# Node one-hots of a graph kernel's edge passes: made by ScalarE, two groups ahead, in place of VectorE

## The chip, the cores and the metric

The kernel runs on one core of a Trainium2 chip. The metric is the device time in microseconds (us) of one execution, the median of several.

## What is computed

The reference is two layers of a graph network with 3125 nodes of 256 features and 50000 edges, sorted by target node. Each layer adds a graph attention block and a mixing block, and then a mixture of experts. Only the edge passes matter here. The first layer has two of them (one head), the second has one (eight heads). A pass is, in short:

```python
xl = x @ Wl
xr = x @ Wr
xj = xl[src]
h = leaky_relu(xj + xr[dst] + eattr @ We, 0.2)
logits = h @ att
m = segment_max(logits, dst)
ex = exp(logits - m[dst])
alpha = ex / segment_sum(ex, dst)[dst]
out = segment_sum(xj * alpha[:, None], dst)
```

The pass with eight heads takes its logits from three sums per edge and head in place of `h @ att`.

## The kernel before

**Tiles.** Nodes lie in 25 tiles of P = 125 partitions. The edges are cut by a plan, made once at the start, into S = 432 steps. A step holds up to 125 edges whose targets lie in one node tile. G = 16 steps are a group, and a pass runs over NG = 27 groups. `messages` (line 641) is one pass; it is called for the two passes with one head (line 3095) and for the one with eight (line 3138). They are called pass 1, 2 and 3 here.

**One step.** GpSimd gathers the source rows of the step's edges by one indirect DMA (L733). TensorE makes `xr[dst]` as a product of a one-hot matrix with the node tile: the one-hot matrix `oht` has nodes along the partitions and edges along the free dimension (`score`, L939; L949 with eight heads). With one head a second product adds the gathered row (L943), and VectorE takes relu, the weights `att` and the sum in one instruction (`relu`, L778). For the sums by target there is the other one-hot matrix, `oh`, with edges along the partitions (`aggregate`, L985), and VectorE adds each product to the accumulator (`combine`, L869).

**The two one-hot matrices.** `oh` is made by ScalarE (`edge_hots`), one step at a time: the distance of an iota from the edge's target (L1037), then relu(1 - distance) (L1041), 32 instructions a group. `oht` starts as a broadcast: SP loads the targets of the group's 2000 edges into all 125 partitions (L750), and with one head the two edge attributes into two more rows (L752). Then one VectorE instruction per group compares all of it with the partition's own number (`node_hots`, L773) in place, and sets `oht_ready`, for which TensorE waits at the first score of the group. The buffer has RB = 3 slots.

**Softmax.** Per group the logits are turned (`turn_logits`, L956), scanned for maxima by VectorE, and the ends, carries and maxima go through TensorE four more times (L961, L968, L974, L979). VectorE's `arguments` (L837 to L843) releases ScalarE's Exp (`weights`, L1027) and TensorE's `spread_factor` (L979). With one head ScalarE scales the 16 gathered rows (L1048); with eight heads VectorE does that (L850).

**The order of the work.** Each engine runs a sequence written out by hand, and semaphores join them. In body j TensorE takes scores of group j+1 and sums of group j-1 in turn, in eight pairs of steps, with the five turns of group j behind pairs 0 to 4. VectorE goes through k = 0 to 15: relu of group j+1, combine of group j-1, and between them `own_maxima` (k = 1), `carries` (3), `maxima` (5), `arguments` (8); at k = 9 stand `node_hots` for group j+2 and `take_sources` (L142), which hands the source numbers of group j+3 to GpSimd. With eight heads `scale` follows at k = 12 to 15. The body ends with `logits` of group j+1. ScalarE's body j is Exp, scales, the factor (L1031), and `edge_hots` of group j+1. SP loads the `oht` of group j+3 when the scores of group j are done and the maxima of group j are ready. GpSimd gathers group g in four blocks, each behind the sums of that block of group g-3.

**The start of a pass.** VectorE makes the first three `take_sources`, then node_hots of groups 0 and 1, then clears the accumulator (L902). ScalarE begins with `edge_hots` of group 0.

Of the kernel before, what the change touches and what calls it, by code (L numbers as in the profile page):

```python
# [15 lines left out]
ALU = mybir.AluOpType  # L16
ACT = mybir.ActivationFunctionType
# [3 lines left out]
P = 125  # L21
# [7 lines left out]
NG = S // G  # L29
RB = 3  # L30
# [109 lines left out]
def copy_ts(nc, out, in_):  # L140

    return nc.vector.tensor_scalar(out, in_, 1.0, None, ALU.mult)  # L142
# [498 lines left out]
def messages(nc, name, call, c, table, heads, dst_rows, edge_lin, att, acc, marks, ee):  # L641
# [12 lines left out]
    with Stage(nc, name) as st:  # L654
# [3 lines left out]
        oht = st.sb("oht", [K1, RB, G * P])  # L658
# [27 lines left out]
        hots_landed = [st.sem(f"hots_landed{q}") for q in range(RB)]  # L686
        pens_landed = [st.sem(f"pens_landed{q}") for q in range(RB)]
        oh_ready = st.sem("oh_ready")
        oht_ready = st.sem("oht_ready")
        dist_ready = st.sem("dist_ready")  # L690
        z_ready = st.sem("z_ready")
        z_used = st.sem("z_used", credit=3)
        lg_ready = st.sem("lg_ready")
# [14 lines left out]
        hots_in = 48 if one else 32  # L708
        loops = (NG - 3) // RB

        def at_steps(g, n=G):
            return bass.ds(g * G, n)
# [8 lines left out]
        with st.block() as block:  # L721
# [43 lines left out]
            def _(dve):  # L765
                ch = Chain(dve, order)

                def take_sources(g, u):
                    copy_ts(nc, cur[:, u % RB, :], c.src_s[:, at_steps(g)]).then_inc(slot_ready.sem, 1)

                def node_hots(g, u, lap):
                    dve.wait_ge(hots_landed[u % RB].sem, hots_landed[u % RB].at(lap * hots_in + hots_in))
                    nc.vector.tensor_scalar(oht[0:P, u % RB], oht[0:P, u % RB], c.part[0:P, 0:1], None, ALU.is_equal).then_inc(oht_ready.sem, 1)  # L773

                def relu(g, u, k):
                    if k % 2 == 0:
# [75 lines left out]
                def node_tiles(g, half):  # L852
                    return load_row(nc, mybir.EngineType.DVE, c.nt_row[0:1, bass.ds(g * G + half * (G // 2), G // 2)], NT)

                def rescale(g, u, nt):
                    dve.wait_ge(fac_ready.sem, fac_ready.at(g + 1))
                    dve.wait_ge(combined.sem, combined.at(g * G))
                    if one:
                        a_t = acc[:, bass.ds(nt, 1), 0:W].rearrange("p a f -> p (a f)")
                        ch(nc.vector.tensor_scalar(a_t, a_t, fac[:, u % RB, 0:1], None, ALU.mult))  # L860
                    else:
                        a_t = acc[:, bass.ds(nt, 1), :].rearrange("p a (h f) -> p (a h) f", h=heads)
                        ch(nc.vector.tensor_tensor(a_t, a_t, fac[:, u % RB].unsqueeze(2).broadcast_to([P, heads, dr + 1]), ALU.mult))
# [7 lines left out]
                def body(j, u, i, first=False, final=False, spare=True):  # L871
                    nts = None
                    for k in range(G):
                        if not first and k % (G // 2) == 0:
                            nts = node_tiles(j - 1, k // (G // 2))
                        if not first and k == 0:
                            rescale(j - 1, u - 1, nts[0])
                        if one and not final:
                            relu(j + 1, u + 1, k)
                        if not first:  # L880
                            combine(j - 1, u - 1, k, nts[k % (G // 2)])
                        if k == 1:
                            own_maxima(j, u, i + u // RB)
                        if k == 3:
                            carries(j)
                        if k == 5:
                            maxima(j, u)
                        if k == 8:
                            arguments(j, u)
                        if k == 9 and not final and spare:  # L890
                            node_hots(j + 2, u + 2, i + (u + 2) // RB)
                            take_sources(j + RB, u)
                        if not one and k in (12, 13, 14, 15):
                            scale(j, u, k - 12)
                    if not final:
                        logits(j + 1, u + 1, i + (u + 1) // RB)

                for q in range(RB):
                    take_sources(q, q)
                node_hots(0, 0, 0)  # L900
                node_hots(1, 1, 0)
                ch(nc.vector.memset(acc[:], 0.0))  # L902
                nc.vector.memset(carry[:], -BIG)
                ch(nc.vector.memset(ends_row[:], -BIG))
# [118 lines left out]
            @block.scalar  # L1023
            def _(act):
                def weights(g, u):
                    act.wait_ge(arg_ready.sem, arg_ready.at(g + 1))
                    nc.scalar.activation(ex[:, u % RB], arg[:], ACT.Exp).then_inc(ex_ready.sem, 1)  # L1027

                def factors(g, u):
                    act.wait_ge(facp_ready.sem, facp_ready.at(g + 1))  # L1030
                    nc.scalar.activation(fac[:, u % RB], facp, ACT.Exp).then_inc(fac_ready.sem, 1)  # L1031

                def edge_hots(g, u):

                    for k in range(G + 1):
                        if k < G:
                            nc.scalar.activation(dist[:, k % 4, :], c.iota[0:P, 0:P], ACT.Abs, scale=-1.0, bias=c.rel[:, bass.ds(g * G + k, 1)]).then_inc(dist_ready.sem, 1)  # L1037
                        if k == 0:
                            continue
                        act.wait_ge(dist_ready.sem, dist_ready.at(g * G + k))  # L1040
                        last = nc.scalar.activation(oh[:, u % RB, k - 1, :], dist[:, (k - 1) % 4, :], ACT.Relu, scale=-1.0, bias=c.ones[0:P, 0:1])  # L1041
                    last.then_inc(oh_ready.sem, 1)

                def scale(g, u, k):
                    if k == 0:
                        act.wait_ge(ex_ready.sem, ex_ready.at(g + 1))
                    r = rows[:, u % RB, k, 0:W]
                    nc.scalar.activation(r, r, ACT.Copy, scale=ex[:, u % RB, k:k + 1]).then_inc(scaled.sem, 1)  # L1048

                def body(j, u, final=False):  # L1050
                    weights(j, u)
                    if one:
                        for k in range(4):
                            scale(j, u, k)
                    factors(j, u)
                    if one:
                        for k in range(4, G):
                            scale(j, u, k)
                    if not final:
                        edge_hots(j + 1, u + 1)  # L1060

                edge_hots(0, 0)
                body(0, 0)
                for i in range(loops):
                    for u in range(1, RB + 1):
                        body(i * RB + u, u)
                body(NG - 2, NG - 2)
                body(NG - 1, NG - 1, True)

# [2148 lines left out]
```

## Time and profile before

| | us |
|---|---|
| runs (three) | 5356.63, 5372.47, 5395.53 |
| median | 5372.47 |
| profiled execution | 5395.91 |
| its span | 5394.1 |
| TensorE matmul busy | 4372.8 (81%) |
| VectorE busy | 2810.2 (52%) |
| ScalarE busy | 2150.7 (40%) |
| GpSimd busy | 1957.3 (36%) |

The profile is one execution. PE is TensorE's matmuls, PEld its weight loads, DVE is VectorE, ACT is ScalarE, POOL is GpSimd, SP is SyncE and SPq its queue. L773 is line 773 of the kernel. Times are in us from the start of the span unless marked ns. "<-" behind an idle time names what ended it; "issue" is time in which an engine waited for nothing that the profile shows. The clock of TensorE is given as a share of 2.4 GHz. A float32 matmul of the program is two instructions. The three edge passes lie at about 1604 to 2330, 2546 to 3265 and 3930 to 4670 us.

### The profile page before, as it was taken

The numbers are of one execution on the slowest core, as the hardware profiler recorded it, in microseconds if no ns is written. First come the engines' busy times: TensorE is split into PE (matmuls) and PEld (weight loads), VectorE is DVE, ScalarE is ACT, GpSimd is POOL, SyncE is SP. The second block draws the span as 40 slices with busy tenths as digits, with TensorE's granted clock in tenths as the row PEclk, the third lists the DMA queues.
The fourth block names the chain that finished last, engine by engine and source line by source line (L and its number), as shares of the span: only waits on it lengthen the run. The fifth ranks groups of instructions, "written<-read, shape, count | busy, mean of one in ns | idle before, by whom it ended". The sixth has DMA issues, their size and how long they took to land. (4 is left out here: it accounts for less than half of the span.)

```text
span 5394.1 us, 74052 instructions
## 1 busy us (share of the span) xinstructions
PE 4372.8 (81%) x22063; PEld 3643.8 (68%) x22064; DVE 2810.2 (52%) x8470; ACT 2150.7 (40%) x6545; POOL 1957.3 (36%) x1544
## 2 busy tenths in 40 slices
PE   9499999999968989986889998389468888556694
PEld 9379888797856777754677775379346666345694
DVE  2262542626316666634666663643547677628424
ACT  2244434445334566623466662323433343121222
POOL 0000000000008777701887771056268888200141
PEclk9799999999989999967999996589656666677697
DMA  5510000000025555412555543632666666210613
GB/s 136 155 43 1 17 10 18 10 1 17 10 67 124 125 125 123 113 39 51 120 130 123 121 112 72 173 113 69 135 139 133 137 139 133 68 43 5 212 35 85
DMA packets 371044, 469.79 MB, mean 87 GB/s; under 512 B 166216, under 2 KB 303417, under 8 KB 370208
## 3 DMA queue, kind: packets, MB, share of 16 engines
q1 hardware_dynamic: 178964, 264.68, 19.4%
q0 software_dynamic: 191744, 200.92, 17.1%
q8 instruction: 175, 2.87, 0.2%
q14 instruction: 161, 1.32, 0.1%
HBM read 399.94 MB, written 63.87 MB: 86 GB/s over the span
## 5 line engine op out<-in xcount | busy, mean ns | idle before, releaser
L733 POOL DMA_INDIRECT msg_rows<-tab_d,msg_cur x1296 | 1646.0, 1270 | 1781.5 <-DVE msg_cur L142 1361.3
L985 PE MATMUL msg_agp<-msg_rows,msg_oh 125*125 125x261 f32 (+2 forms) x2592 | 848.5, 457 | 15.4 <-DVE ga_acc L869 7.0
L985 PEld LDWEIGHTS msg_agp<-msg_rows,msg_oh 125*125 125x125 f32 x2592 | 548.1, 223 | 128.3 <-issue 22.6
L939 PE MATMUL msg_zp<-g_xr,msg_oht 127*125 x1728 | 547.2, 398 | 80.4 <-DVE msg_oht L773 63.3
L943 PE MATMUL msg_zp<-msg_rows,c_ident 125*125 125x256 f32 x1728 | 527.0, 386 | 37.4 <-DMA msg_rows<-tab_d,msg_cur 37.4
L778 DVE SCALAR_TENSOR_TENSOR msg_hid<-msg_zp,g_att 125x256 f32<-125x256 f32 x864 | 360.5, 420 | 316.0 <-PE msg_zp L943 208.4
L1037 ACT ACTIVATE msg_dist<-c_iota,c_rel 125x125 f32<-125x125 f32 x1296 | 493.0, 387 | 48.8 <-PEq L3020 33.9
L1041 ACT ACTIVATE msg_oh<-msg_dist,c_ones 125x125 f32<-125x125 f32 x1296 | 493.2, 387 | 0.0
L1027 ACT ACTIVATE msg_ex<-msg_arg 125x16 f32<-125x16 f32 (+1 forms) x81 | 20.0, 247 | 1020.7 <-DVE msg_delta L843 829.3
L869 DVE TENSOR_TENSOR gv_acc<-gv_acc,msg_agp 125x261 f32 (+1 forms) x864 | 364.3, 422 | 104.4 <-PE msg_agp L985 69.7
L939 PEld LDWEIGHTS msg_zp<-g_xr,msg_oht 127*125 127x125 f32 x1728 | 307.9, 190 | 136.5 <-issue 85.7
L943 PEld LDWEIGHTS msg_zp<-msg_rows,c_ident 125*125 125x125 f32 x1728 | 328.7, 191 | 97.8 <-DMA msg_rows<-tab_d,msg_cur 43.9
L1317 PE MATMUL mix_pb<-mix_ht,mix_w 128*128 128x125 f32 x3200 | 373.5, 275 | 0.0
L1326 PE MATMUL mix_pc<-mix_w,mix_ut 128*125 128x256 f32 x1600 | 361.8, 380 | 7.0 <-ACT mix_ut L1458 7.0
L1317 PEld LDWEIGHTS mix_pb<-mix_ht,mix_w 128*128 128x128 f32 x3200 | 365.6, 192 | 0.4
L1048 ACT ACTIVATE msg_rows<-msg_rows,msg_ex 125x257 f32<-125x257 f32 x864 | 354.2, 497 | 1.7
L1593 DVE TENSOR_TENSOR mix_t<-mix_pc,mix_b 125x256 f32<-125x256 f32 x100 | 42.4, 424 | 543.5 <-PE mix_pc L1326 543.5
L1326 PEld LDWEIGHTS mix_pc<-mix_w,mix_ut 128*125 128x125 f32 x1600 | 292.9, 188 | 47.9 <-issue 8.3
L1279 PE MATMUL mix_pb<-mix_wp,mix_ht 128*125 128x256 f32 x1200 | 282.7, 387 | 4.1 <-ACT mix_ht L1398 4.1
L869 DVE TENSOR_TENSOR ga_acc<-ga_acc,msg_agp 125x264 f32 x432 | 184.4, 427 | 161.0 <-PE msg_agp L985 129.8
L1279 PEld LDWEIGHTS mix_pb<-mix_wp,mix_ht 128*125 128x125 f32 x1200 | 222.6, 192 | 36.4 <-issue 5.5
L1398 ACT ACTIVATE mix_ht<-mix_pa,mix_gb 128x125 f32<-128x125 f32 x208 | 82.8, 450 | 369.2 <-PE mix_pa L1268 369.2
(540 smaller groups left out, 7258.9 us busy)
## 6 DMA issues: line engine op xcount, KB each, us to landing
msg_oht<-rel_d SPq DMA_DIRECT2D x81, 875.0 KB
msg_rows<-tab_d,msg_cur POOLq DMA_INDIRECT x1296
pl_raw<-in_edge_attr SPq DMA_DIRECT2D x25, 448.0 KB
msg_pens<-pen_d SPq DMA_DIRECT2D x270, 31.2 KB
msg_oht<-rel_d SPq DMA_DIRECT2D x81, 101.6 KB
mix_w<-in_L_mix_W SPq DMA_DIRECT2D x8, 1024.0 KB
m0w_wr<-in_L_ffn_w SPq DMA_DIRECT2D x16, 512.0 KB
m0w_w2r<-in_L_ffn_w SPq DMA_DIRECT2D x16, 512.0 KB
```

Source lines behind the costliest of these rows:

```text
L733: nc.gpsimd.indirect_dma_start(out=rows[:, q, k, :], out_offset=None, in_=table, in_offset=bass.IndirectOffsetOnAxis(ap=cur[:, q, k:k + 1] ...
L778: last = nc.vector.scalar_tensor_tensor(out=hid[:, k, :], in0=zp[:, pair_bank(u, k // 2), (k % 2) * D:(k % 2 + 1) * D], scalar=0.0, in1=at ...
L869: nc.vector.tensor_tensor(a_t, a_t, agp[:, sum_bank(u, k), 0:AW], ALU.add).then_inc(combined.sem, 1)
L939: nc.tensor.matmul(z, hots, d_t, start=True, stop=False)
L943: last = nc.tensor.matmul(z, c.ident[0:P, 0:P], rows[:, u % RB, k, 0:D], start=False, stop=True)
L985: nc.tensor.matmul(agp[:, sum_bank(u, k), 0:AW], oh[:, u % RB, k, :], rows[:, u % RB, k, 0:AW], start=True, stop=True).then_inc(summed.sem, 1)
L1037: nc.scalar.activation(dist[:, k % 4, :], c.iota[0:P, 0:P], ACT.Abs, scale=-1.0, bias=c.rel[:, bass.ds(g * G + k, 1)]).then_inc(dist_ready ...
L1041: last = nc.scalar.activation(oh[:, u % RB, k - 1, :], dist[:, (k - 1) % 4, :], ACT.Relu, scale=-1.0, bias=c.ones[0:P, 0:1])
L1048: nc.scalar.activation(r, r, ACT.Copy, scale=ex[:, u % RB, k:k + 1]).then_inc(scaled.sem, 1)
L1279: last = nc.tensor.matmul(pb[bank][0:P, lo:lo + D], ht[:, t % HR, kc, :], wp[:, w, kc, :], start=(kc == 0), stop=(kc == 1))
L1317: last = nc.tensor.matmul(out, w1[:, kc, f * 128:(f + 1) * 128], ht[:, t % HR, kc, :], start=(kc == 0), stop=(kc == 1))
L1326: last = nc.tensor.matmul(pc[t % 2][0:P, 0:D], ut[:, t % 2, f, :], w2[:, f, :], start=(f == 0), stop=(f == FC - 1))
```

## The change

`node_hots` moves from VectorE to ScalarE. VectorE's comparison is replaced by two ACTIVATEs over the same 125x2000 elements, in place: the absolute value of (partition number - target), and relu(1 - that). The second waits on a new semaphore, `far_ready`, for the first. ScalarE makes the one-hots of group j+2 at the head of its body j, ahead of the Exp of group j; at the start of a pass it makes those of group 0, then the edge one-hots of group 0, then the node one-hots of group 1. The wait for the load (`hots_landed`) goes with it. VectorE's `take_sources` stays where it was.

```diff
--- before.py
+++ after.py
@@ -688,6 +688,7 @@
         oh_ready = st.sem("oh_ready")
         oht_ready = st.sem("oht_ready")
         dist_ready = st.sem("dist_ready")
+        far_ready = st.sem("far_ready")
         z_ready = st.sem("z_ready")
         z_used = st.sem("z_used", credit=3)
         lg_ready = st.sem("lg_ready")
@@ -767,10 +768,6 @@
 
                 def take_sources(g, u):
                     copy_ts(nc, cur[:, u % RB, :], c.src_s[:, at_steps(g)]).then_inc(slot_ready.sem, 1)
-
-                def node_hots(g, u, lap):
-                    dve.wait_ge(hots_landed[u % RB].sem, hots_landed[u % RB].at(lap * hots_in + hots_in))
-                    nc.vector.tensor_scalar(oht[0:P, u % RB], oht[0:P, u % RB], c.part[0:P, 0:1], None, ALU.is_equal).then_inc(oht_ready.sem, 1)
 
                 def relu(g, u, k):
                     if k % 2 == 0:
@@ -888,7 +885,6 @@
                         if k == 8:
                             arguments(j, u)
                         if k == 9 and not final and spare:
-                            node_hots(j + 2, u + 2, i + (u + 2) // RB)
                             take_sources(j + RB, u)
                         if not one and k in (12, 13, 14, 15):
                             scale(j, u, k - 12)
@@ -897,8 +893,6 @@
 
                 for q in range(RB):
                     take_sources(q, q)
-                node_hots(0, 0, 0)
-                node_hots(1, 1, 0)
                 ch(nc.vector.memset(acc[:], 0.0))
                 nc.vector.memset(carry[:], -BIG)
                 ch(nc.vector.memset(ends_row[:], -BIG))
@@ -1041,6 +1035,14 @@
                         last = nc.scalar.activation(oh[:, u % RB, k - 1, :], dist[:, (k - 1) % 4, :], ACT.Relu, scale=-1.0, bias=c.ones[0:P, 0:1])
                     last.then_inc(oh_ready.sem, 1)
 
+                def node_hots(g):
+
+                    act.wait_ge(hots_landed[g % RB].sem, hots_landed[g % RB].at((g // RB + 1) * hots_in))
+                    h = oht[0:P, g % RB]
+                    nc.scalar.activation(h, h, ACT.Abs, scale=-1.0, bias=c.part[0:P, 0:1]).then_inc(far_ready.sem, 1)
+                    act.wait_ge(far_ready.sem, far_ready.at(g + 1))
+                    nc.scalar.activation(h, h, ACT.Relu, scale=-1.0, bias=c.ones[0:P, 0:1]).then_inc(oht_ready.sem, 1)
+
                 def scale(g, u, k):
                     if k == 0:
                         act.wait_ge(ex_ready.sem, ex_ready.at(g + 1))
@@ -1048,6 +1050,8 @@
                     nc.scalar.activation(r, r, ACT.Copy, scale=ex[:, u % RB, k:k + 1]).then_inc(scaled.sem, 1)
 
                 def body(j, u, final=False):
+                    if j + 2 < NG:
+                        node_hots(j + 2)
                     weights(j, u)
                     if one:
                         for k in range(4):
@@ -1059,7 +1063,9 @@
                     if not final:
                         edge_hots(j + 1, u + 1)
 
+                node_hots(0)
                 edge_hots(0, 0)
+                node_hots(1)
                 body(0, 0)
                 for i in range(loops):
                     for u in range(1, RB + 1):
```

## Rows read from the trace of the kernel before

**Rows 1.** The passes: length; PE, PEld, DVE, ACT, POOL busy; clock, DMA share, GB/s.
```profile
1604.00:2330.00 726.00, 634.89 (x2915) 506.04 (x2915) 467.67 (x1960) 434.17 (x1351) 542.81 (x432) 0.96 0.54 118
2546.00:3265.00 719.00, 630.55 (x2917) 502.62 (x2917) 464.09 (x1935) 434.51 (x1351) 541.50 (x432) 0.96 0.53 119
3930.00:4670.00 740.00, 592.15 (x2079) 447.67 (x2079) 506.49 (x1245) 264.35 (x919) 561.72 (x432) 0.62 0.58 127
```

**Rows 2.** Timeline of one group of pass 2: start, us, engine, line, operation, count, idle before.
```profile
2903.16 1.16 SPq L750 DMA_DIRECT2D msg_oht<-rel_d  x2
...
2907.65 0.34 PE L979 MATMUL msg_m<-msg_delta,msg_oh 1*125 1x1 f32 x2 [0.88 <-issue]
...
2907.84 1.86 POOL L733 DMA_INDIRECT msg_rows<-tab_d,msg_cur  x1 [0.30 <-issue]
...
2908.10 1.24 DVE L773 TENSOR_SCALAR msg_oht<-msg_oht,c_part 125x2000 f32<-125x2000 f32 x1
...
2912.56 0.42 DVE L778 SCALAR_TENSOR_TENSOR msg_hid<-msg_zp,g_att 125x256 f32<-125x256 f32 x1 [0.84 <-issue]
...
2918.45 0.27 PE L956 MATMUL msg_m<-c_ident,msg_lg 125*16 125x125 f32 x1
```

**Rows 3.** Single instructions: ns min/median/max, first and last start.
```profile
L773 DVE TENSOR_SCALAR msg_oht<-msg_oht,c_part x81: 1242/1245/1687, 1611.2 to 4600.9; 125x2000 f32<-125x2000 f32 x81
...
L1037 ACT ACTIVATE msg_dist<-c_iota,c_rel x1296: 382/386/401, 1604.5 to 4636.3; 125x125 f32<-125x125 f32 x186
...
L1048 ACT ACTIVATE msg_rows<-msg_rows,msg_ex x864: 492/497/514, 1654.9 to 3263.7; 125x257 f32<-125x257 f32 x173
...
L733 POOL DMA_INDIRECT msg_rows<-tab_d,msg_cur x1296: 1207/1211/7077, 1605.6 to 4622.7; - x186
...
L750 SPq DMA_DIRECT2D msg_oht<-rel_d x162: 4/332/748, 1604.7 to 4571.6; - x162
```

**Rows 4.** ScalarE in pass 2: timeline, and its waits from 2610 to 3230.
```profile
2922.93 0.67 ACT L1041 ACTIVATE msg_oh<-msg_dist,c_ones 125x125 f32<-125x125 f32 x2
...
2932.52 0.22 ACT L1027 ACTIVATE msg_ex<-msg_arg 125x16 f32<-125x16 f32 x1 [8.91 <-DVE msg_delta L843]
...
2749.78 0.22 ACT L1027 ACTIVATE msg_ex<-msg_arg 125x16 f32<-125x16 f32 x1 [7.72 <-DVE msg_delta L843]
...
ACT msg_ex L1027 <- DVE msg_delta L843: 148.5, 16, 11.6
```

**Rows 5.** Timeline of VectorE in two groups of pass 3.
```profile
4343.96 0.43 DVE L869 TENSOR_TENSOR ga_acc<-ga_acc,msg_agp 125x264 f32 x1 [0.87 <-PE msg_agp L985]
...
4368.18 1.24 DVE L773 TENSOR_SCALAR msg_oht<-msg_oht,c_part 125x2000 f32<-125x2000 f32 x1
...
4371.03 0.43 DVE L869 TENSOR_TENSOR ga_acc<-ga_acc,msg_agp 125x264 f32 x1 [0.33 <-DVE ga_acc L869]
```

**Rows 6.** Timeline of GpSimd and VectorE at the start of pass 3.
```profile
3972.81 7.08 POOL L733 DMA_INDIRECT msg_rows<-tab_d,msg_cur  x1 [0.30 <-issue]
...
3974.05 4.75 DVE L850 TENSOR_TENSOR msg_rows<-msg_rows,msg_ex 125x1056 f32<-125x1056 f32 x4
...
3989.39 0.37 DVE L795 TENSOR_TENSOR msg_lg<-msg_zp,msg_rows 125x128 f32<-125x128 f32 x1 [10.59 <-DMA msg_rows<-tab_d,msg_cur]
```

**Rows 7.** TensorE's waits for gathered rows: 1604 to 1700, 2546 to 2740, 2740 to 3265.
```profile
PEld msg_zp L943 <- DMA msg_rows<-tab_d,msg_cur: 18.4, 3, 13.6
...
PEld msg_zp L943 <- DMA msg_rows<-tab_d,msg_cur: 24.6, 10, 12.5
...
PEld msg_zp L943 <- DMA msg_rows<-tab_d,msg_cur: 0.3, 1, 0.3
```

**Rows 8.** Timeline of ScalarE in pass 3: three successive Exps.
```profile
4210.92 0.31 ACT L1027 ACTIVATE msg_ex<-msg_arg 125x128 f32<-125x128 f32 x1 [16.53 <-DVE msg_delta L843]
...
4235.76 0.31 ACT L1027 ACTIVATE msg_ex<-msg_arg 125x128 f32<-125x128 f32 x1 [14.91 <-issue]
...
4262.77 0.31 ACT L1027 ACTIVATE msg_ex<-msg_arg 125x128 f32<-125x128 f32 x1 [16.86 <-DVE msg_delta L843]
```

## The prediction

> **What bounds the kernel now.** The views were read in this order: the busy shares of the three edge passes, the durations of single instructions, one steady group on all engines, the waits, and the starts of the passes.
>
> In the three passes [rows 1] TensorE is the busiest engine (635 of 726 us, 631 of 719, 592 of 740), GpSimd follows (543, 542, 562), VectorE has 468, 464 and 506, ScalarE 434, 435 and 264. A share does not say who sets the pace, so take one steady group of pass 2 [rows 2]. TensorE runs the last turn of group 12 (L979) at 2907.65 and the first turn of group 13 (L956) at 2918.45. Between them lie 10.80 us of scores and sums with hardly a gap. The same stretch, read group by group, is 10.8 to 11.1 us in 19 of 26 groups of pass 2 and 10.84 us in 19 of pass 1. So it is TensorE's own work. VectorE's node_hots (L773) sits inside this stretch, at 2908.10, for 1.24 us. After it VectorE catches up, and at 2912.56 it has stood idle for 0.84 us again. What costs the groups time beyond TensorE's work are the turns before L979, where TensorE waits for VectorE (L979 itself 0.88 us here), and node_hots comes behind all of these in program order.
>
> Two more things are to be seen. The gather that meets node_hots takes 1.86 us [rows 2], where the median is 1.211 [rows 3]. And at the start of a pass TensorE waits for gathered rows: 18.4 us in three waits in pass 1, 24.6 us in ten in pass 2, but only 0.3 us in the rest of pass 2 [rows 7].
>
> **Removed from VectorE.** 81 instructions (27 groups in three passes) with a median of 1.245 us [rows 3]: at least 101 us of VectorE. In passes 1 and 2 all of it is covered by the stretch that TensorE fills. If that cover were gone, 54 x 1.25 = 67 us would be the price. In pass 3 the tail of a group is VectorE's (scale, sums, logits), and TensorE waits for the logits, so the question is whether node_hots delays that tail. Two kinds of groups alternate there. In one, TensorE runs at its half clock (the granted mean is 0.62 in [rows 1], between 1.2 and 2.4 GHz), and VectorE's next sum waits 0.87 us for TensorE after node_hots. In the other, VectorE does node_hots at 4368.18, take_sources and two sums, and then is idle for 0.33 us before the sum at 4371.03 that opens the tail [rows 5]. That sum needs a TensorE product that started after 4370. So both kinds are covered, the second one narrowly: without node_hots the two sums come earlier, the third does not. I take 0 here; the bounds are 0 and 27 x 1.24 = 33 us.
>
> Outside these, in a group of passes 1 and 2 whose sources or turns come late, VectorE may have less slack than usual. The stretch L979 to L956 is above 11.1 us in 12 groups of passes 1 and 2. Some of these are TensorE at its half clock after a long gap and some are waits for gathers. For what VectorE's relief gives there I take 1 us, between 0 and 12 x 1.25 = 15.
>
> **Added to ScalarE.** Two dependent ACTIVATEs over 125x2000 in place of one comparison. The trace has no ACTIVATE of that size. The rows for 125 and 257 elements are 0.386 and 0.497 us [rows 3], which is 0.84 ns per element, so 2000 elements come to 0.497 + 1743 x 0.00084 = 1.96 us. That is an estimate from the slope of two short rows. The second waits for the end of the first; with a handover of under 0.1 us, an estimate, a pair is 4.0 us, 81 of them 324 us more ScalarE. From below a pair is 2 x 0.497 = 1.0 us; from above I allow the rate of the slope twice, 7.8 us.
>
> Where does it lie? ScalarE's order becomes: edge_hots(j), then node_hots(j+2), then the Exp of group j, its scales, edge_hots(j+1). In the trace ScalarE ends edge_hots at 2923.60 and idles 8.91 us until the Exp is released by VectorE [rows 4]. Over the middle of pass 2 such waits are 148.5 us in 16, 9.3 on average; the smallest among groups that get the new work is 7.72 [rows 4]. In pass 3 it is 14.9 to 16.9 us [rows 8]. So 4.0 us fits everywhere, and even the upper bound of 7.8 is over the smallest wait by 0.1 only. What is queued behind the new waits is the Exp, for which the scales, then TensorE's sums wait; but those are wanted only at the next group.
>
> The wait for the broadcast load moves with it. SP issues that load at 2903.16 [rows 2] for the group that ScalarE would prepare at 2923.60, 20 us later. The first load of the kernel is issued at 1604.7 and releases VectorE at 1611.2 [rows 3], 6.5 us with three loads in flight. Such a load has long landed. The engine past which the wait is moved is ScalarE alone; SP's and GpSimd's queues keep their order. TensorE wants the result a whole group later than ScalarE now makes it. At the start of a pass the first one-hots come 2.7 us later (4.0 in place of 1.24), but TensorE then waits for the first gathered rows anyway, by the longest wait of [rows 7], 13.6 and 12.5 us. ScalarE's own first edge one-hots move by some 11 us, and they are used a whole group later. I count 0.
>
> take_sources comes 1.24 us earlier; the indices it writes are read a group later, so 0. VectorE's clearing of the accumulator starts some 15 us earlier in each pass, under the same wait for rows: 0.
>
> **What GpSimd gets back.** A gather that met node_hots lost 0.65 us. ScalarE's ACTIVATEs do not do this: twelve gathers of this group run under edge_hots and scales at 1.21. In steady groups this is worth nothing, since TensorE waits 0.3 us for rows over 525 us [rows 7]. At the start it is worth what GpSimd has saved when TensorE waits for it for the last time. Pass 1: two stretched gathers before that, 1.3 us. Pass 2: the waits beyond the unavoidable first are 24.6 - 12.5 = 12.1 us, spread over about seven groups, and seven gathers give back 4 us by then. Pass 3: one gather took 7.08 us because node_hots and four scales of 4.75 us followed each other, and VectorE then waited 10.59 us for those rows [rows 6]; the 1.24 us goes, and 0.9 of two earlier gathers, 2.1 in all. Sum 7.4; bounds 0 and 81 x 0.65 = 53.
>
> By the page "SBUF — State Buffer" of the Trainium skill, section "SBUF: two separate sides", a VectorE instruction in a two-port mode locks GpSimd out of a port pair that they share, and a gather issued from GpSimd then cannot write its descriptors, while ScalarE has its own ports. The 1.86 us beside 1.21 agrees with it.
>
> **The sum.** 7.4 + 1 = about 8 us off the profiled execution's 5395.9 us (span 5394.1): 5387.9. That execution lies 23.4 us above the median of the runs shown, 5372.5, so the forecast for the median is 5364.5. The three runs alone spread over 39 us (0.7%); within 1% is about what a measurement of this kernel can tell from no change.
>
> **Rivals.**
> *GpSimd sets the pace everywhere.* Then each stretched gather is worth its 0.65 us: 53 us, 5319. For it: GpSimd is three quarters busy and 16 gathers with their gaps (1.21 and 0.30 us, [rows 2, 3]) take 24.2 of the 26.6 us that a group of pass 2 has, its start included. Against it: TensorE's waits for rows end after the first groups [rows 7]. This is what the page's rule on the shared ports would make of the time if descriptors were the limit. Chance 0.08.
> *VectorE sets the pace.* All 81 count, 101 us, 5271; or those of pass 3 alone, 33 us, 5339. For it: TensorE and VectorE wait for each other at every turn. Against it: the constant 10.80 us and the idle time behind node_hots. Chance 0.06 for all, 0.04 for pass 3 alone.
> *ScalarE becomes the bound (slower).* A group of passes 1 and 2 has 16 us of ScalarE work (434 / 27) in 26.6. The place is the Exp behind the pair. It decides from a pair of 7.7 us on, if the long ACTIVATEs run far below the slope or a load lands late; at 10 us a pair, the Exp is late by 2 us or less in most groups, and if that went straight to TensorE, 54 x 1.0 to 54 x 2.3 us, say 80, 5452. Against it: the slope, and a whole group of slack behind the Exp. Chance 0.03.
> The Trainium skill's page "ScalarE: Activation LUTs", section "Rules for kernel authors", speaks against the change: element by element arithmetic belongs on VectorE. The durations agree (1.245 beside 4.0 us); if the engine's own time counted, 81 x 2.75 = 223 us would be lost. The idle ScalarE makes that rule idle here.
> *The clock falls otherwise (slower).* In pass 3 groups of 24.84 and 27.01 us follow each other [rows 8], with TensorE at its full clock in a part of the one and at half in the other; some 10 are short and 15 long. If all became long, 10 x 2.2 = 22 us, 5386. Chance 0.04, and as much for all short, 15 x 2.2 = 33 us less, 5331; here the direction is open.
>
> **Chances and range.** Forecast 0.71, the rivals as given, sum 1.00. Faster by over 1% (below 5319): the 0.06 and half of the 0.08, 0.10. Slower by over 1%: 0.03. Within: 0.87. The range goes from 5322, which takes in pass 3 alone and the fast clock, to 5398, which takes in the slow clock and the spread of the runs.
>
> **What would show it.** L773 gone from VectorE; two ACTIVATEs of 125x2000, each 1.9 to 2.0 us; ScalarE's wait before the Exp smaller by 4 us (about 5.5 in pass 2, 12 in pass 3) and never zero; L979 to L956 still 10.80; gathers stretched in pass 2 gone, and GpSimd waiting more for TensorE's sums; TensorE's waits for rows in pass 2's first groups shorter by about 4 us. The prediction is wrong if the stretch L979 to L956 shrinks, if pass 3's groups lose a microsecond each, or if the Exp starts right behind the pair.

## The result, and the profile after

The changed kernel took 5317.11 us (median of four executions, 5309.05 to 5331.9), the kernel before 5371.33 (5356.63 to 5395.53). The ratio is 0.9898, with a 95% interval of 0.9854 to 0.9942: 54 us faster. The prediction said 5364.5 us with a range of 5322 to 5398, so the time lies 5 us below the range. It lies within 2 us of the rival "GpSimd sets the pace everywhere" (5319 us), which had a chance of 0.08. On which chip, or chips, these first runs were made is not on record; later runs, below, show that this matters. The profiled execution of the changed kernel took 5331.9 us beside 5395.9 before.

The three passes after, in the columns of [rows 1]:

```profile
1614.00:2312.00 698.00, 635.35 (x2943) 502.96 (x2943) 442.43 (x1952) 537.55 (x1405) 524.39 (x432) 0.97 0.55 123
2517.00:3215.00 698.00, 632.94 (x2948) 503.06 (x2948) 438.12 (x1927) 537.79 (x1406) 524.68 (x432) 0.97 0.56 122
3870.00:4603.00 733.00, 589.21 (x2079) 447.23 (x2079) 469.13 (x1219) 367.63 (x973) 541.14 (x432) 0.62 0.59 128
```

The windows are 28, 21 and 7 us shorter than in [rows 1], but their ends were set by hand. From the first to the last turn of the logits, which is the measure used from here on, the passes shrank from 668.6, 662.9 and 673.0 us to 630.4, 631.6 and 666.7. So the gain is in passes 1 and 2. GpSimd's busy time is 524 us in each of them, which is 432 gathers at 1.21 us. It was 542.

The one-hots on ScalarE, single instructions as in [rows 3]:

```profile
L1042 ACT ACTIVATE msg_oht<-msg_oht,c_part x81: 1945/1948/1962, 1621.1 to 4520.2; 125x2000 f32<-125x2000 f32 x81
...
L1044 ACT ACTIVATE msg_oht<-msg_oht,c_ones x81: 1961/1962/1967, 1623.1 to 4522.2; 125x2000 f32<-125x2000 f32 x81
```

One steady group of pass 2, as in [rows 2] (L973 is the turn that was L979, L950 the one that was L956, L734 the gather, L775 the relu):

```profile
2888.79 0.34 PE L973 MATMUL msg_m<-msg_delta,msg_oh 1*125 1x1 f32 x2 [0.80 <-DVE msg_delta L840]
...
2889.80 1.21 POOL L734 DMA_INDIRECT msg_rows<-tab_d,msg_cur  x1 [0.30 <-issue]
...
2891.10 0.42 DVE L775 SCALAR_TENSOR_TENSOR msg_hid<-msg_zp,g_att 125x256 f32<-125x256 f32 x1 [1.64 <-PE msg_zp L937]
2891.32 1.21 POOL L734 DMA_INDIRECT msg_rows<-tab_d,msg_cur  x1 [0.30 <-issue]
...
2899.59 0.27 PE L950 MATMUL msg_m<-c_ident,msg_lg 125*16 125x125 f32 x1
```

The gathers follow each other at 1.51 us without a break: 16 of them are 24.2 us, and the groups of passes 1 and 2 now follow each other at 24.3 and 24.4 us, where it was 25.9 and 25.7. TensorE's stretch from L973 to L950 is 10.80 us in this group, as before.

Now the waits in the steady part of pass 1, from 1700 to 2280 us (us in total, times, longest). First the changed kernel:

```profile
ACT msg_ex L1021 <- DVE msg_delta L840: 108.8, 24, 7.6
...
PEld msg_zp L937 <- DMA msg_rows<-tab_d,msg_cur: 16.1, 20, 1.6
PE msg_zp L937 <- DMA msg_rows<-tab_d,msg_cur: 8.5, 12, 1.2
...
POOL msg_rows L734 <- PE msg_agp L979: 4.9, 16, 0.3
```

Then the kernel before, in the same window:

```profile
DVE msg_hid L778 <- remote: 26.3, 26, 2.4
POOL msg_rows L733 <- PE msg_agp L985: 21.8, 34, 3.4
```

After the change TensorE waits for gathered rows in nearly every group, and GpSimd waits for nobody (0.3 us is its gap anyway). GpSimd is the pace. In the profile before it was the other way round: TensorE did not wait for rows [rows 7], and GpSimd waited for sums. The row "remote" is one that the prediction passed over. VectorE's relu began up to 2.2 us after TensorE's pair had ended by its record and VectorE was free, and no instruction of the profile accounts for it (the views call some of these waits "remote" and some "issue"). Such starts, called late starts here where they are over 0.3 us, came 94 times in groups 1 to 25 of passes 1 and 2 in the profile before, and not once in the one after.

### The profile page after: what moved, and what is told of

Its sections match the earlier page's. It is cut to its first block and busy times, and to the rows that moved or that the text cites. A ratio compares the mean times of both kernels' runs of the same rounds, so it can differ in the third digit from the quotient of the medians.

```text
span 5330.1 us, 74136 instructions
## 1 busy us (share of the span) xinstructions
PE 4367.9 (82%) x22063; PEld 3641.8 (68%) x22064; DVE 2705.4 (51%) x8389; ACT 2461.3 (46%) x6707; POOL 1904.0 (36%) x1544
## 5 line engine op out<-in xcount | busy, mean ns | idle before, releaser
L734 POOL DMA_INDIRECT msg_rows<-tab_d,msg_cur x1296 | 1590.2, 1227 | 1768.9 <-DVE msg_cur L142 1367.0
L979 PE MATMUL msg_agp<-msg_rows,msg_oh 125*125 125x261 f32 (+2 forms) x2592 | 845.3, 456 | 15.3 <-DVE ga_acc L866 11.8
L979 PEld LDWEIGHTS msg_agp<-msg_rows,msg_oh 125*125 125x125 f32 x2592 | 547.5, 222 | 124.9 <-DVE ga_acc L866 18.4
L775 DVE SCALAR_TENSOR_TENSOR msg_hid<-msg_zp,g_att 125x256 f32<-125x256 f32 x864 | 360.8, 420 | 386.3 <-PE msg_zp L937 381.8
```

What stands on the lines that cost most here:

```text
L734: nc.gpsimd.indirect_dma_start(out=rows[:, q, k, :], out_offset=None, in_=table, in_offset=bass.IndirectOffsetOnAxis(ap=cur[:, q, k:k + 1] ...
L775: last = nc.vector.scalar_tensor_tensor(out=hid[:, k, :], in0=zp[:, pair_bank(u, k // 2), (k % 2) * D:(k % 2 + 1) * D], scalar=0.0, in1=at ...
L979: nc.tensor.matmul(agp[:, sum_bank(u, k), 0:AW], oh[:, u % RB, k, :], rows[:, u % RB, k, 0:AW], start=True, stop=True).then_inc(summed.sem, 1)
```

## Experiments

Theory G: GpSimd's gathers set the pace of passes 1 and 2, and the comparison cost what it held up the gathers. Theory V: VectorE's own 1.25 us a group cost it. Theory C came later: the late starts belong to the chip. The ratio is to executions of the kernel before on the same chip at the same time. "First to last turn" is given for passes 1, 2 and 3 of each profile.

| run | chip | ratio to the kernel before (95%) | late starts | first to last turn, us |
|---|---|---|---|---|
| before, first profile | not on record | | 94 | 668.6, 662.9, 673.0 |
| after, first profile | not on record | 0.9898 (0.9854 to 0.9942) | 0 | 630.4, 631.6, 666.7 |
| v_same | 3 | 0.9984 (0.9968 to 0.9999) | 0 | 647.4, 645.3, 672.7 |
| v_psum | 3 | 0.9944 (0.9926 to 0.9961) | 0 | 628.9, 628.8, 684.8 |
| g_fill | 3 | 0.9919 (0.9903 to 0.9936) | 0 | 630.1, 633.3, 663.3 |
| b_stt | 3 | 1.0054 (1.0037 to 1.0071) | 0 | 666.0, 666.0, 667.7 |
| before_again | 1 | 1.0006 (0.9990 to 1.0022) | 98 | 669.7, 665.8, 673.5 |
| after_again | 1 | 0.9982 (0.9963 to 1.0001) | 92 | 657.3, 655.9, 665.1 |
| g_mem | 1 | 0.9888 (0.9862 to 0.9914) | 46 | 644.3, 644.0, 667.3 |
| g_fifteen | 1 | 0.9862 (0.9834 to 0.9889) | 50 | 622.0, 622.7, 680.9 |
| before_third | 11 | 0.9997 (0.9976 to 1.0018) | 78 | 666.6, 655.1, 669.8 |
| after_third | 11 | 0.9970 (0.9954 to 0.9986) | 101 | 661.8, 659.7, 660.1 |
| g_mem_again | 11 | 0.9927 (0.9901 to 0.9953) | 45 | 643.6, 643.7, 670.1 |
| layout | 11 | 0.9983 (0.9965 to 1.0001) | 85 | 663.4, 662.2, 666.2 |
| before_fourth | 11 | 1.0015 (0.9994 to 1.0036) | 116 | 671.1, 672.5, 669.8 |
| after_fourth | 11 | 0.9969 (0.9952 to 0.9986) | 111 | 656.2, 656.4, 662.9 |
| b_mem | 11 | 0.9969 (0.9953 to 0.9985) | 54 | 660.2, 657.9, 670.8 |
| g_mem_third | 11 | 0.9905 (0.9874 to 0.9935) | 51 | 645.0, 642.6, 661.1 |

The kernel before had a median of 5364 us on chip 3, 5398 on chip 1, and on chip 11, which was used at two times, 5386 and 5400. One profile is one execution: the part of the program ahead of the first gather of pass 1, which no experiment touches, took between 1599 and 1632 us in these profiles. So a difference of a whole profiled execution says less than one of the passes.

### What of the comparison cost the time: v_same, v_psum, b_stt

The edits here and below are shortened to the lines that matter.

```diff
--- after
+++ v_same, VectorE at k == 9 ahead of take_sources
+                    if one:
+                        flat = hid[:].rearrange("p k d -> p (k d)")[:, 0:G * P]
+                        nc.vector.tensor_scalar(flat, flat, c.part[0:P, 0:1], None, ALU.is_equal)
--- after
+++ v_psum, relu
+                    for n in range(3 if k == 9 else 0):
+                        nc.vector.scalar_tensor_tensor(out=hid[:, n, :], in0=zp[:, pair_bank(u, 4), D:2 * D], scalar=0.0, in1=att[:], op0=ALU.max, op1=ALU.mult)
--- before
+++ b_stt, node_hots
-                    nc.vector.tensor_scalar(oht[0:P, u % RB], oht[0:P, u % RB], c.part[0:P, 0:1], None, ALU.is_equal)
+                    nc.vector.scalar_tensor_tensor(out=oht[0:P, u % RB], in0=oht[0:P, u % RB], scalar=c.part[0:P, 0:1], in1=c.ones[0:P, 0:1].broadcast_to([P, G * P]), op0=ALU.is_equal, op1=ALU.mult)
```

Expected of v_same: 

> The changed kernel, with an idle comparison of the same form and size (tensor_scalar, 125x2000, SBUF to SBUF, 1.24 us) put back on VectorE at k = 9 in passes 1 and 2; nothing waits for it. Theory G (GpSimd's gathers set the pace of passes 1 and 2; the comparison held them up 0.65 us a group) and theory V (VectorE's own 1.25 us a group in its chain set it) both expect most of the gain of passes 1 and 2 gone: 2 x 35 us, so about 5317 + 60 = 5377 us (5360 to 5385). Under G the trace shows one gather per group of 1.7 to 2.1 us again. If neither holds, and the gain came from the one-hots being ready elsewhere or earlier, the time stays at 5317 us.

Expected of v_psum: 

> The changed kernel, with three idle relu-like instructions (125x256 from PSUM, 0.42 us each, 1.26 us in all) on VectorE ahead of its relu at k = 9 in passes 1 and 2. VectorE loses as much time as the comparison cost, but by a form beside which no gather of the trace was longer than 1.21 us. Theory G: no change, 5317 us (5310 to 5325), all gathers 1.21 us. Theory V: as the run with the comparison, about 5377 us.

Expected of b_stt: 

> The kernel before, with the same comparison made in another form (scalar_tensor_tensor with a broadcast one as the second operand), estimated at 2.1 us in place of 1.24 us at one element a cycle. Theory G: if this form doesn't hold up the gathers, the stretched ones (0.65 us a group) are gone and the time falls by 50 us or less, to 5320 to 5345 us, although VectorE works longer; if it holds them up for longer, the time grows by 54 times the extra stretch, up to 45 us, 5415 us. Theory V: slower by 54 x 0.9 = 48 us, 5420 us, whatever the gathers do. The durations of the gathers beside it tell G's two cases apart.

Measured: v_same 5356.95 us, v_psum 5333.29, b_stt 5395.68. The timelines of the three, in this order:

```profile
2881.11 2.19 POOL L734 DMA_INDIRECT msg_rows<-tab_d,msg_cur  x1 [0.30 <-issue]
2881.71 1.24 DVE L772 TENSOR_SCALAR msg_hid<-msg_hid,c_part 125x2000 f32<-125x2000 f32 x1
```

```profile
2891.64 1.06 DVE L776 SCALAR_TENSOR_TENSOR msg_hid<-msg_zp,g_att 125x256 f32<-125x256 f32 x3
2892.07 1.21 POOL L734 DMA_INDIRECT msg_rows<-tab_d,msg_cur  x1 [0.30 <-issue]
```

```profile
2886.12 2.28 DVE L773 SCALAR_TENSOR_TENSOR msg_oht<-msg_oht,c_part,c_ones 125x2000 f32<-125x2000 f32 x1
2887.19 2.30 POOL L733 DMA_INDIRECT msg_rows<-tab_d,msg_cur  x1 [0.30 <-issue]
```

An instruction for which nothing waits brought back 17 and 14 us in passes 1 and 2, and the groups went from 24.3 to 24.95 us. The expectation of 60 us more was sized from the first pair of profiles, in which only one has late starts; 33 us more than g_fill were measured. Its gathers were longer by 0.75 us for each comparison. VectorE's work without the hold-up (1.06 us as executed) cost passes 1 and 2 nothing: 628.9 and 628.8 us, beside 630 to 633 without it. So theory V falls there. The median of v_psum is 9 us above g_fill's and outside what G expected (5310 to 5325). Where these 9 us lie is not shown: the two profiled executions are only 2 us apart, with pass 3, the same code in both, 21 us longer in v_psum and the part ahead of pass 1 15 us shorter. The other form of the comparison does not help, for each of its 54 instances in passes 1 and 2 held up the gathers beside it by 1.45 us on average, and the groups followed at 25.67 us, which is 24.2 + 1.45. Its slower time alone fits V as well as G; the spacing is what speaks for G, and TensorE's waits. From 1700 to 2280 us TensorE and its weight loads waited for gathered rows for 21 us in g_fill, 22 in v_psum, 49 in v_same and 67 in b_stt, while GpSimd waited for nobody in any of the four.

By the page "SBUF — State Buffer" of the Trainium skill, section "SBUF: two separate sides", the ports that VectorE shares with GpSimd are taken by a two-port mode, and not by an instruction with at most one SBUF input outside those modes; an instruction with two SBUF inputs is only in the way of a GpSimd instruction that reads SBUF. The timelines of v_same (2.19 us) and v_psum (1.21 us) agree with the first two cases. b_stt is the third, and its gather took 2.30 us; a gather takes its source numbers from `cur` in SBUF, which would fit, but no run here separates that read from the writing of descriptors.

### Making GpSimd slower and faster: g_fill, g_mem, g_fifteen

```diff
--- after
+++ g_fill, gather
+                    for _ in range(10 if one else 0):
+                        pool.sem_inc(filled.sem, 1)
--- after
+++ g_mem, gather, for each block b
+                        if one and b % 2 == 1:
+                            pool.wait_ge(filled.sem, filled.at(2 * g + (b + 1) // 2))
+                        if one and b % 2 == 0:
+                            nc.gpsimd.memset(spare_t[:], 0.0).then_inc(filled.sem, 1)
--- after
+++ g_fifteen, gather and SP's load
-                        for k in range(b * QS, (b + 1) * QS):
+                        for k in range(b * QS, min((b + 1) * QS, G - 1)):
...
+                    if not first:
+                        sp.wait_ge(summed.sem, summed.at((g - RB) * G + G))
+                    sp.dma_start(rows[:, q, G - 1, :], table[0:P]).then_inc(fixed[q].sem, 16)
```

In g_mem the unused output of the relu, hid, is one row shorter, which makes the room for spare_t, and VectorE does one small memset more at the start of passes 1 and 2. g_fifteen leaves out the sources of one step in 16, so it tells about time alone; the waits for the gathers are changed to match.

Expected of g_fill: 

> The changed kernel, with ten idle semaphore increments on GpSimd ahead of each group's gathers in passes 1 and 2, estimated at 0.03 to 0.07 us each, 0.3 to 0.7 us a group. Theory G: GpSimd's cycle grows by just that, and the time by 54 times it: 16 to 38 us, 5333 to 5355 us, and the spacing of the groups at TensorE grows from 24.3 us by what the gather's spacing shows. Theory V: nothing, 5317 us.

Measured 5323.92 us. The gathers stayed at 24.2 us a group, so the increments lay beside the gathers and the run tells nothing about GpSimd. It serves as the changed kernel on chip 3, where that kernel itself was not run: 43 us (5364 x 0.0081) faster than the kernel before, 33 us faster than v_same.

Expected of g_mem: 

> The changed kernel, with two idle memsets of 125x256 on GpSimd in each group of passes 1 and 2 (0.31 us each by the one of that size in the trace), since the semaphore increments of the last attempt took none of its time: the gathers of a group stayed at 24.2 us. Theory G: the group of gathers grows from 24.2 to 24.8 us or a little more, the spacing at TensorE by the same, and the time by 54 x 0.62 = 33 us, to about 5350 us beside 5317 for the changed kernel. Theory V (VectorE's own time): no change.

Expected of g_fifteen: 

> The changed kernel with 15 gathers a group in place of 16, in all three passes: the last step of each group gets its rows by one plain transfer of the first 125 rows of the table, issued by SP, so that step's sources are left out. Theory G: GpSimd's group falls from 24.2 to 22.7 us; TensorE waited for rows 33 us in 25 groups of pass 1, so passes 1 and 2 go on to about 23.0 us a group and the time falls by 54 x 1.2 = 65 us or more, to 5230 to 5260 us. Theory V, or TensorE's own work: less than 10 us.

Measured: g_mem 5334.67 us, on a chip where the unchanged copy of the changed kernel took 5383.37. Its groups follow at 24.84 and 24.80 us, as theory G says of GpSimd's slower cycle (24.2 + 0.6). Yet the kernel with more work ran 49 us faster than the one without. In the two profiles 25 us of this lie in passes 1 and 2, and 17 ahead of pass 1, where no memset runs. g_fifteen took 5325.34 us: passes 1 and 2 lost 33 to 35 us each beside after_again, which G wants, but pass 3 grew by 16 us and the groups stopped at 24.0 to 24.2 us in place of the expected 23.0, so the expected 5230 to 5260 was missed by 65 us. Both results need the next part.

### The same kernels again: late starts

Expected of before_again: 

> The kernel before, unchanged, for a second profile. In the first one VectorE's relu began late by 0.3 us or more after TensorE's pair 47 times in each of passes 1 and 2 (42 and 45 us in all), and GpSimd waited 17 and 10 us for sums. If both belong to the kernel, they come again, with GpSimd's gathers of a pass spread over 680 to 690 us. If they belonged to that execution, the gathers spread over some 672 us, as in the run with the idle comparison, and the groups follow at 24.9 to 25.0 us.

Expected of after_again: 

> The changed kernel, unchanged, for a second profile and a closer ratio: 0.990 of the kernel before (0.988 to 0.992), groups of passes 1 and 2 at 24.2 to 24.4 us, no gather over 1.25 us in them, and pass 3 within 10 us of the first profile's.

The ratio of 0.990 was not repeated: 5383.37 us beside 5398.15. The late starts were in both kernels. Two later pairs were run to see whether they go with the kernel or with the chip.

Expected of before_third: 

> The kernel before, for a third profile. Theory C (the late starts of VectorE's relu, by which a TensorE pair is seen 0.6 to 2.1 us after its end, belong to some chips and not to the kernel): where the profile shows none of them, the groups of passes 1 and 2 follow at 24.9 to 25.0 us, set by GpSimd (16 gathers of 1.51 us and 0.65 to 0.75 us of stretch), and the profiled span is 5350 to 5370 us; where it shows 40 or more a pass, it is the first profile again. If they belong to the kernel before, they are there on every chip.

Expected of after_third: 

> The changed kernel, for a third profile and a ratio on the same chip as the run above. Theory C: without late starts in the profile the ratio is 0.990 to 0.993 and the groups follow at 24.3 us; with them the ratio is 0.997 to 0.999, as in the second profile (where GpSimd waited 23 us a pass for sums, which took back what the stretches had cost).

Expected of before_fourth: 

> The kernel before, for a fourth profile. Theory C (late starts belong to the chip): none in the profile and groups of passes 1 and 2 at 24.9 to 25.0 us, or 35 to 50 a pass and groups at 25.3 to 25.9 us; the run of the changed kernel in the same call shows the same kind. If instead the late starts belong to the kernel before, they are here and not in the changed one.

Expected of after_fourth: 

> The changed kernel on the same chip. Theory C: without late starts a ratio of 0.990 to 0.993 and groups at 24.3 us; with them 0.996 to 0.999 and groups at 25.3 to 25.6 us.

Measured: before_third 5388.0, after_third 5370.31, before_fourth 5411.99, after_fourth 5381.02 us. All twelve profiles from chips 1 and 11 have late starts, and none of the four from chip 3 has; the changed kernel has none in one profile and 92 to 111 in three. So they do not come with the change, and they go with the chip as far as three chips can show (two of them were used at one time only). A profile of the kernel before without them was not had. The recorded semaphore updates go with them: 38 to 41 thousand in the profiles with late starts, 54 to 55 thousand in those without. By both signs the first profile of the kernel before (39.6 thousand) is like those of chips 1 and 11, and the first of the changed kernel (54.4 thousand) like those of chip 3. So the first 54 us may in part be a difference between two chips. This is a late start, in the timeline of after_fourth, pass 2:

```profile
2758.01 0.59 PE L937 MATMUL msg_zp<-msg_rows,c_ident 125*125 125x256 f32 x2
...
2758.44 1.03 PE L979 MATMUL msg_agp<-msg_rows,msg_oh 125*125 125x258 f32 x4
...
2759.84 0.23 PE L962 MATMUL msg_m<-c_ones,msg_cin_row 1*16 1x1 f32 x4 [0.36 <-DVE msg_cin_row L821]
...
2760.53 1.21 POOL L734 DMA_INDIRECT msg_rows<-tab_d,msg_cur  x1 [0.30 <-issue]
...
2761.14 0.42 DVE L775 SCALAR_TENSOR_TENSOR msg_hid<-msg_zp,g_att 125x256 f32<-125x256 f32 x1 [1.44 <-remote]
```

TensorE's pair ended at 2758.60 and it began its next turn at 2759.84, but VectorE got the pair at 2761.14. In the first profile of the kernel before, nearly all late starts lie either 0.6 or 1.3 to 1.5 us behind the start of a gather (here 0.61). That GpSimd's work delays the news of TensorE's results, or that TensorE itself is behind its modelled ends, would both look so; which it is stays open.

What they do to the change is in the waits of after_fourth, pass 1, 1700 to 2280 us:

```profile
DVE msg_hid L775 <- remote: 50.5, 42, 1.6
POOL msg_rows L734 <- PE msg_agp L979: 19.0, 35, 2.6
POOL msg_rows L734 <- remote: 14.3, 14, 1.2
```

GpSimd's gathers are all 1.21 us, but it waits again for sums that come late: beyond its gap of 0.3 us, 19.0 + 14.3 - 49 x 0.3 = 18.6 us in this window. Over the whole of passes 1 and 2 together, GpSimd's waits beyond its gap are 20 to 36 us in the four profiles of the kernel before and 48 to 56 in the three of the changed one with late starts, while its gathers are 38 to 43 us shorter in sum. So about half of what the change gave back to GpSimd is waited away. The change is then worth 0.2 to 0.3% by the ratios; the medians of before_fourth and after_fourth alone are 31 us apart.

### Pauses of GpSimd: g_mem_again, layout, b_mem, g_mem_third

layout is g_mem without the memsets and their waits; b_mem is the kernel before with g_mem's lines.

Expected of g_mem_again: 

> The changed kernel with two idle memsets of 125x256 on GpSimd in each group of passes 1 and 2 (and one row fewer in the unused output of VectorE's relu), which ran 0.9% faster than the changed kernel on a chip with late starts. On such a chip, if it was the pauses or the layout: again 5330 to 5340 us against 5375 to 5390 us. On a chip without late starts theory G expects 33 us more than the changed kernel.

Expected of layout: 

> The kernel of the run above without the memsets: the same tiles at the same places, one small memset of VectorE more at the start of passes 1 and 2. Where late starts occur: if the pauses of GpSimd reduced them, this one runs as the changed kernel (ratio 0.997 to 0.999); if the layout did, as the one with memsets or faster (0.985 to 0.989). Where none occur: as the changed kernel, within 5 us.

Expected of b_mem: 

> The kernel before with the two idle memsets on GpSimd in each group of passes 1 and 2. Theory G: where late starts are few, GpSimd's group is 24.2 + 0.6 (memsets) + 0.65 (stretch) = 25.45 us and TensorE follows at that, 0.65 us a group or 35 us behind the run with memsets and without the comparison, on any chip. If the pauses help by themselves on a chip with late starts, this kernel has half as many late starts as the kernel before and runs as it or up to 0.5% faster; on a chip without them it is 33 us slower than the kernel before.

Expected of g_mem_third: 

> The changed kernel with the two idle memsets, on the same chip: groups at 24.8 us. On a chip with late starts 25 to 50 us faster than the changed kernel; on a chip without them 33 us slower than it. 35 us faster than the kernel before with memsets on either.

Measured: g_mem_again 5345.46, layout 5381.02, b_mem 5385.25, g_mem_third 5346.48 us. So the pauses do it and not the place of the tiles. They cut the late starts to 45 to 54, passes 1 and 2 together are 25, 34 and 25 us shorter than in the changed kernel's profiles beside them, and they help the kernel before too, by 0.3%. The waits of g_mem_third, in the same window, show the pace back at GpSimd:

```profile
DVE msg_hid L781 <- remote: 16.4, 13, 1.4
POOL msg_rows L740 <- POOL msg_spare L735: 7.4, 41, 0.2
...
POOL msg_rows L740 <- PE msg_agp L987: 5.6, 20, 0.3
```

With GpSimd as the pace on both sides, the change is worth 5385.25 - 5346.48 = 39 us on chip 11 too; passes 1 and 2 are 15 us shorter each, which is 26 groups by 0.6 us, and pass 3 by 10. On the chips with late starts g_mem is the fastest of the complete kernels, 25 to 49 us ahead of the changed one. It was not run on a chip without them; there theory G makes it 33 us slower.

## Why the prediction was wrong

- **The step that failed**: "In steady groups this is worth nothing, since TensorE waits 0.3 us for rows over 525 us [rows 7]." The row was right for that execution, but the reason was not that GpSimd had slack: late starts held TensorE and VectorE back just as much. GpSimd's 24.2 us of gathers, about 0.7 us of hold-up and its waits for sums made 25.6 and 25.3 us a group (its gathers spread over 689.5 and 681.4 us in passes 1 and 2), as much as TensorE's groups took. Where the late starts are away, the hold-up is on the path in every group of passes 1 and 2: 33 us between the medians of g_fill and v_same, 29 of them in these two passes by the profiles. The prediction had the sum that says so (24.2 of 26.6 us) and set it aside as a rival. It also made GpSimd's room look wider than it was: 26.6 us has the start of the pass in it, while steady groups of pass 2 followed at 25.7 us, of which GpSimd's gathers with the hold-up took 24.9.
- **What the 54 us are.** On chip 3, where the like of it is 43 us, 33 us are the held-up gathers of passes 1 and 2 and the rest is what v_same, which has no comparison in pass 3, still gains on the kernel before (0.16%, 9 us, with an interval of 1 to 17). The first ratio's interval reaches to 0.9942; whether its other 11 us are more than the spread or come from the chip, no run shows. That the time fell within 2 us of the rival's 5319 is luck in part: the rival priced all 81 gathers at 0.65 us, and 27 of them are in pass 3. In the first two profiles a part of the difference (38 and 31 us in passes 1 and 2, where v_same differs from after by 17 and 14) is that one had late starts and the other had none.
- **VectorE's cover** held. Its work may come and go in the stretch behind L979 without an effect on passes 1 and 2 (v_psum). L979 to L956, forecast to stay at 10.80 us, has 11.5 us on average in place of 11.2, since TensorE now waits there for rows. GpSimd, forecast to wait more for TensorE's sums, waited less: on the run without late starts not at all.
- **ScalarE** was right: 1.948 and 1.962 us beside the estimated 1.96, a wait before the Exp of 5.2 us on average and never under 3.6 in passes 1 and 2, and 12.1 in pass 3 (predicted 5.5 and 12). The Trainium skill's rule in "ScalarE: Activation LUTs", section "Rules for kernel authors", which prices the engine's own time, decided nothing here: the cost of the VectorE instruction lay on a third engine.
- **The start of a pass** stayed: from the first gather to the first turn 39.1 and 38.7 us in pass 1, 37.0 and 37.0 in pass 2, 33.7 and 33.3 in pass 3. The 7.4 us booked there were not there; in passes 1 and 2 the saving came later, spread over the groups.
- **Pass 3** gave 6 us in the first pair of profiles and 7 to 10 in the others, against a forecast of 2 us and a bound of 33. The clock rival did not show as priced, but see below.
- The forecast of 8 us is what the change was worth on chips 1 and 11 within a few us (10 to 17 by the ratios). That is luck and does not make it right: the reason given for it was GpSimd's slack, and the profile had a row against it ("remote") that was not read.

## What to carry to other kernels

An instruction can cost more by what it locks out than by its own time: look for the longest instances of the neighbour's instructions (1.86 us beside a median of 1.21) and add them up against the neighbour's whole cycle, not against its waits in one profile. If an engine's cycle is within a few per cent of the group's, a profile in which it also waits for others does not show slack: the engines may wait for each other in a ring, and time taken from it counts once the others run smoothly. Read the rows that name no instruction as their releaser before giving a wait to an engine, and run the pair again on another chip before a gain of one per cent is believed.

## What the hardware did unexpectedly

Idle memsets on GpSimd, 0.33 us each, two a group, made kernels faster where late starts occur: by 25 to 49 us the changed kernel on chips 1 and 11, and by 15 the kernel before on chip 11. The late starts were halved and not gone, and they hardly occur at k = 0 (at most 4 in a profile, none in the kernel before) and behind k = 8 (at most 7), where the groups of [rows 2] have the turn L979. The same profiles also have fewer semaphore updates recorded, as said above; no cause is shown for either.

Pass 3 runs at a mixed TensorE clock. These are the windows of pass 3 for g_fill, v_psum and b_stt, in the columns of [rows 1]:

```profile
3867.00:4595.00 728.00, 588.74 (x2079) 447.14 (x2079) 468.33 (x1216) 367.68 (x973) 539.93 (x432) 0.62 0.60 129
```

```profile
3851.00:4600.00 749.00, 614.07 (x2079) 467.98 (x2079) 469.17 (x1216) 367.58 (x973) 542.58 (x432) 0.59 0.57 125
```

```profile
3936.00:4668.00 732.00, 568.09 (x2079) 421.98 (x2079) 525.99 (x1244) 264.27 (x919) 561.38 (x432) 0.66 0.58 128
```

The first two are the same code in this pass, and they differ by 21 us with the granted clock at 0.62 and 0.59 of 2.4 GHz; the same 2079 matmuls were busy for 589 and 614 us. The third has 57 to 58 us more of VectorE's work, a clock of 0.66 and nearly the time of the first. So what pass 3 gains from a change of 1 us a group (27 us) is hardly more than these 21 us, by which two executions of the same code differ.
